# Two-head attention in value blocks of four steps, row maxima half a group ahead, and projection loads moved

## The reference

```
h = layernorm(x, g1, be1) * (1 + scale_msa) + shift_msa
q, k, v = split(h @ Wqkv + bqkv)                       # (B, S, H, HD) each
attn = softmax(einsum('blhd,bmhd->bhlm', q, k) * HD**-0.5, axis=-1)
h = einsum('bhlm,bmhd->blhd', attn, v).reshape(B, S, D) @ Wproj + bproj
x = x + gate_msa * h
x = x + gate_mlp * mlp(layernorm(x, g2, be2) * (1 + scale_mlp) + shift_mlp)
```

## Time and profile before

| | |
|---|---|
| the profiled execution's own time | 3572.36 us |
| its span | 3570.6 us |
| mean granted TensorE clock | 0.949 |
| TensorE matmul busy | 3329.7 us (93%) |
| VectorE busy | 2006.8 us (56%) |
| GpSimd busy | 1573.1 us (44%) |
| ScalarE busy | 1537.6 us (43%) |
| attention, first load to last store | about 886 to 2603 us |
| projection | about 2604 to 2845 us |

### The profile page before, as it was taken

One profiled execution on the slowest core, in us unless ns is written; L12 is line 12 of the kernel. 1 busy time (PEld: TensorE's weight loads), 2 busy tenths in 40 slices (PEclk: granted clock), 3 DMA queues, 4 the chain that ended last, 5 costly groups with the idle time before them and its releaser, 6 DMA issues. The chain is left out here.

```text
span 3570.6 us, 45393 instructions
## 1 busy us (share of the span) xinstructions
PE 3329.7 (93%) x17036; PEld 2237.9 (63%) x17036; DVE 2006.8 (56%) x3384; ACT 1537.6 (43%) x2790; POOL 1573.1 (44%) x590
## 2 busy tenths in 40 slices
PE   7989996998899999999999999999946699999999
PEld 6478885777455555555555555554324478888887
DVE  1278884443887877787777877775033332222222
ACT  0011113443056666666666666667613342222222
POOL 1033331000067887788777878778834200000000
PEclk9899997999599999999999999999967899999999
DMA  4222223444446776667766776666655431111100
GB/s 153 85 80 94 93 86 138 171 169 151 104 110 159 184 170 163 162 160 177 183 167 167 168 178 164 162 150 144 145 158 193 169 132 39 39 39 38 38 33 24
DMA packets 200487, 458.89 MB, mean 129 GB/s; under 512 B 61419, under 2 KB 83179, under 8 KB 169582
## 3 DMA queue, kind: packets, MB, share of 16 engines
q1 hardware_dynamic: 142126, 265.59, 22.3%
q0 software_dynamic: 18432, 134.23, 18.5%
q10 hardware_dynamic: 39744, 56.63, 6.1%
HBM read 165.71 MB, written 88.34 MB: 71 GB/s over the span
## 5 line engine op out<-in xcount | busy, mean ns | idle before, releaser
L1226 DVE TENSOR_REDUCE att_mx<-att_pM 128x1 f32<-128x512 f32 x2048 | 1249.4, 681 | 328.8 <-PE att_pM L1281 328.3
L1211 ACT ACTIVATE att_prob<-att_pS 128x512 f32<-128x512 f32 x2048 | 1040.3, 620 | 440.3 <-PE att_pS L1328 438.9
L1153 POOL TENSOR_TENSOR att_acc<-att_acc,att_prob 128x2048 f32<-128x2048 f32 x224 | 1029.8, 4597 | 204.5 <-ACT att_prob L1211 192.1
L1281 PE MATMUL att_pM<-att_ks,att_qs 96*128 96x512 f32 x2048 | 843.5, 426 | 21.3 <-DMA att_ks<-qk_d 21.2
L1328 PE MATMUL att_pS<-att_qs,att_ks 98*128 98x512 f32 x2048 | 844.3, 416 | 4.0 <-ACT att_prob L1211 3.7
L1328 PEld LDWEIGHTS att_pS<-att_qs,att_ks 98*128 98x128 f32 x2048 | 384.7, 189 | 350.1 <-issue 203.2
L1296 PE MATMUL att_pO<-att_prob,att_V 128*32 128x512 f32 x4096 | 497.4, 603 | 0.0
L1281 PEld LDWEIGHTS att_pM<-att_ks,att_qs 96*128 96x128 f32 x2048 | 404.7, 198 | 129.3 <-DVE att_mx L1226 52.4
L1782 DVE TENSOR_TENSOR mlp_us<-mlp_tu,mlp_us 128x512 fp32r<-128x512 f32 x128 | 89.7, 701 | 536.9 <-ACT mlp_us L1755 536.9
L1825 PE MATMUL mlp_pu<-mlp_hs,mlp_W 128*128 128x512 f32 x1536 | 371.1, 391 | 19.6 <-DVE mlp_W L1774 19.6
L1844 PE MATMUL mlp_pa<-mlp_W,mlp_us 128*128 128x512 f32 x1536 | 368.8, 389 | 0.0
(11 more groups left out here) (197 smaller groups left out, 3037.8 us busy)
## 6 DMA issues: line engine op xcount, KB each, us to landing
att_gathered<-att_prob POOLq DMA_DIRECT2D x128, 1024.0 KB, 7.9
att_gathered<-att_prob SPq DMA_DIRECT2D x64, 1024.0 KB, 4.7
qk_d<-qkv_qs SPq DMA_DIRECT2D x64, 512.0 KB, 2.7
att_qs<-qk_d ACTq DMA_DIRECT2D x39, 512.0 KB, 8.4
att_ks<-qk_d ACTq DMA_DIRECT2D x39, 512.0 KB, 7.5
gat_xT<-in_xT SPq DMA_DIRECT2D x32, 256.0 KB, 3.2
gat_xrow<-in_x SPq DMA_DIRECT2D x32, 256.0 KB, 2.8
x_d<-gat_x SPq DMA_DIRECT2D x32, 256.0 KB, 2.1
```

Source lines behind the costliest of these rows:

```text
L1153: nc.gpsimd.tensor_tensor(acc[half][:], old[:], new[:], ALU.add).then_inc(added, 1)
L1211: nc.scalar.activation(prob[step % PR][:, c, :], pS[at % 3][:], ACT.Exp, scale=SCALE).then_inc(exp_done, 1)
L1226: nc.vector.tensor_reduce(mx[:, q // 4, q % 4:q % 4 + 1], bank(at)[:], AX.X, ALU.max).then_inc(m_read, 1)
L1281: nc.tensor.matmul(bank(at)[:], qs[k][0:KD, h, t * P:(t + 1) * P], ks[k][0:KD, h, mc * 512:(mc + 1) * 512], start=True, stop=True).then_in ...
```

## The change

In attention: the values of four steps are made together (VB = 4) instead of two. The maxima are organised by half groups (n = 2g + half, NM = 64 tiles), and run half a group and six steps ahead, so that 64 + 24 tiles come before the first score and the first half of the last group still has maxima; `top_of`, `parts` and `rows` come twice per group, with 16 rows instead of 32, and `rows` is four DMAs instead of two. q and k have two buffers instead of three; their loads for group g + 1 are issued at steps 1, 2, 3, 5, 6 and 7 of group g, and V at step 8. Group 0's loads are split by head. In the memory that is freed, projection's weights, bias, gates and first chunk are loaded while attention runs. In projection, `of` and `zr` of chunk i + 2 are loaded when chunk i's low part is made; `xr` still behind chunk i's store.

```diff
-        NM = 2 * MT * 4
+        NM = MT * 4
-        U = 3
+        U = 2
+        VB = 4
-        LOADS = [3, 6, 9, 12, 15, 18]
+        LOADS = [1, 2, 3, 5, 6, 7]
...
         def m_tile(g, step, c):
-            ahead = 1 if step < ST - LEAD else 2
-            return (g + ahead, (step + LEAD) % ST * 4 + c) if g + ahead < NG else None
+            n, at = 2 * g + step // MT, step % MT
+            ahead = 1 if at < MT - LEAD else 2
+            return (n + ahead, (at + LEAD) % MT * 4 + c) if n + ahead < 2 * NG else None
...
+        def load_head(eng, h):
+            for i in range(6):
+                if i < 3:
+                    dst, src = qs[0][i * HD:(i + 1) * HD, h], q_v[(0, 0, 1)[i], 0, :, h, 0:S]
+                else:
+                    dst, src = ks[0][(i - 3) * HD:(i - 2) * HD, h], k_v[(0, 1, 0)[i - 3], 0, :, h, 0:S]
+                eng.dma_start(raw(dst), src).then_inc(head_loaded[h], 16)
...
-            def rows(g):
-                sp.wait_ge(m_read, turn(g) + 1)
-                for h in range(2):
-                    sp.dma_start(raw(qs[g % U][KD + h:KD + h + 1]).rearrange("a h (t n) -> a (h t) n", n=P),
-                                 raw(nm[:, h, :])).then_inc(top_rows[g % U], 16)
+            def rows(n):
+                g, half = divmod(n, 2)
+                sp.wait_ge(m_read, turn(n) + 1)
+                for w in range(2):
+                    for h in range(2):
+                        row = qs[g % U][KD + w:KD + w + 1, h, half * (S // 2):(half + 1) * (S // 2)]
+                        sp.dma_start(raw(row).rearrange("a (t n) -> a t n", n=P),
+                                     raw(nm[h * 8:(h + 1) * 8, w, :])).then_inc(top_rows[g % U], 16)
...
-            load(0)
+            load_head(sp, 0)
+            load_head(sp, 1)
+            load_v(0)
             load(1)
-            load_v(0)
             load_v(1)
-            load(2)
             rows(0)
+            for c in range(DC):
+                sp.dma_start(keep["p_stage"][:, c, :], io["Wproj"][c * P:(c + 1) * P, :]).then_inc(weights_early, 16)
...
+                if n == 2 * NG - 2:
+                    sp.wait_ge(o_stored, 64 * (2 * NG - 2))
+                    sp.wait_ge(z_kept, 32 * (2 * NG - 2))
+                    load_output(sp, io, 0, keep["p_of"], keep["p_zr"], first_o, first_z)
...
             def ahead(g, step):
-                if step == 1:
+                if g + 1 == NG:
+                    return
+                if step in LOADS:
+                    load_part(act, g + 1, LOADS.index(step))
+                if step == 8:
                     act.wait_ge(step_done, g * ST)
-                if step == 2 and g + 1 < NG:
                     load_values(act, g + 1)
-                if step in LOADS and g + 2 < NG:
-                    load_part(act, g + 2, LOADS.index(step))
...
-                    if step == ST - LEAD and g + 1 < NG:
-                        top_of(g + 1)
-                    if step == ST - LEAD + 1 and g + 1 < NG:
-                        parts(g + 1)
+                    if step % MT == MT - LEAD and n + 2 < 2 * NG:
+                        top_of(n + 2)
+                    if step % MT == MT - LEAD + 1 and n + 2 < 2 * NG:
+                        parts(n + 2)
...
-                        if c == 2 and step % 2 == 0 and (g or step):
-                            behind(*divmod(g * ST + step - 2, ST))
-                            behind(*divmod(g * ST + step - 1, ST))
+                        if c == 2 and step % VB == 0 and (g or step):
+                            for back in range(VB, 0, -1):
+                                behind(*divmod(g * ST + step - back, ST))
...
 def proj_phase(nc, io, keep):
-            load(0, 0)
...
+            load_o(1, 1)
+            load_x(0, 0)
...
+            load_x(1, 1)
+            for i in range(NCH):
+                s = i % 2
+                if i + 2 < NCH:
+                    sp.wait_ge(o_lo, DC + i)
+                    load_o(i + 2, s)
                 sp.wait_ge(x2_ready, i * 4 + 4)
                 sp.dma_start(io["x2_d"][bass.ds(i * 512, 512), :].rearrange("(n p) d -> p n d", p=P), x2[s][:]).then_inc(x_stored[s], 16)
-                if before(i, NCH - 2):
-                    load(i + 2, s)
+                if i + 2 < NCH:
+                    load_x(i + 2, s)
```

More of the change, by code:

```diff
@@ L1001, in attention_phase @@
             for step in range(ST):
-                if step == ST - LEAD + 1 and g + 1 < NG:
-                    fill(f"turned {g + 1}")
+                n = 2 * g + step // MT + 1
+                if step % MT == MT - LEAD + 1 and n < 2 * NG:
+                    fill(f"turned {n}")
                 for c in range(4):
@@ L1091, in keep_inverted @@
                     sp.dma_start(z_v[g // 2, h, g % 2, half], packed[h * 64:(h + 1) * 64, :]).then_inc(z_kept, 16)
-            load(0)
+            load_head(sp, 0)
+            load_head(sp, 1)
+            load_v(0)
             load(1)
-            load_v(0)
             load_v(1)
-            load(2)
             rows(0)
[L1099 to L1112, removed]
+            for c in range(DC):
+                sp.dma_start(keep["p_stage"][:, c, :], io["Wproj"][c * P:(c + 1) * P, :]).then_inc(weights_early, 16)
+            for b in range(B):
+                sp.dma_start(keep["p_gate"][b][:], io["gate_d"][0, b * (S // 512)]).then_inc(weights_early, 16)
+            sp.dma_start(keep["p_bp"][:], io["rows"][6:7, :].to_broadcast([P, D])).then_inc(weights_early, 16)
+            for n in range(2 * NG):
+                if n >= 1:
+                    store(n - 1)
+                send_first(n)
+                if n >= 1:
+                    pack(n - 1)
+                    keep_inverted(n - 1)
+                if n + 1 < 2 * NG:
+                    rows(n + 1)
+                if n == 2 * NG - 2:
+                    sp.wait_ge(o_stored, 64 * (2 * NG - 2))
+                    sp.wait_ge(z_kept, 32 * (2 * NG - 2))
+                    load_output(sp, io, 0, keep["p_of"], keep["p_zr"], first_o, first_z)
             store(2 * NG - 1)
@@ L1117, in _ @@
             sp.wait_ge(z_kept, 32 * 2 * NG)
+            sp.wait_ge(weights_early, 16 * (DC + B + 1))
+            sp.wait_ge(first_o, 16)
+            sp.wait_ge(first_z, 16 * DC)
         @block.gpsimd
@@ L1273, in _, with maxima, top_of @@
         def _(pe):
[L1274 to L1278, removed]
+            def maxima(n, q):
+                at, (g, half) = place[n, q], divmod(n, 2)
+                k = g % U
+                if n == 0 and q % 32 == 0:
+                    pe.wait_ge(head_loaded[q // 32], 96)
+                if half == 0 and q == 0 and g >= 1:
+                    pe.wait_ge(loaded[k], (g + k) // U * 96)
                 wait_bank(pe, at)
-                h, t, mc = q // 64, q // 4 % MT, q % 4
-                nc.tensor.matmul(bank(at)[:], qs[k][0:KD, h, t * P:(t + 1) * P], ks[k][0:KD, h, mc * 512:(mc + 1) * 512],
+                h, t, mc = q // 32, q // 4 % 8, q % 4
+                nc.tensor.matmul(bank(at)[:], qs[k][0:KD, h, (half * 8 + t) * P:(half * 8 + t + 1) * P], ks[k][0:KD, h, mc * 512:(mc + 1) * 512],
                                  start=True, stop=True).then_inc(m_done, 1)
[L1284 to L1287, removed]
+            def top_of(n):
+                pe.wait_ge(top_ready, n + 1)
+                wait_bank(pe, turn(n))
+                nc.tensor.transpose(bank(turn(n))[0:MT, 0:P], top[:], ident[:]).then_inc(m_done, 1)
             def values(g, step):
@@ L1374, in proj_phase @@
         ones2 = m.sb("ones2", [2, P], F32R)
-        zr = [m.sb(f"zr{i}", [P, DC, 512]) for i in range(2)]
+        zr = [keep["p_zr"], m.sb("zr1", [P, DC, 512])]
         os_ = [m.sb(f"os{i}", [P, 2, DC, 512], F32R) for i in range(2)]
@@ L1379, in proj_phase @@
         xn = m.sb("xn", [P, 4, D])
-        of = [m.sb(f"of{i}", [P, DC, 512]) for i in range(2)]
+        of = [keep["p_of"], m.sb("of1", [P, DC, 512])]
         ht = [m.sb(f"ht{i}", [P, 512]) for i in range(4)]
@@ L1402, in _, with load_o, load_x @@
         def _(sp):
[L1403 to L1412, removed]
-            load(0, 0)
-            sp.dma_start(bp[:], io["rows"][6:7, :].to_broadcast([P, D])).then_inc(b_loaded, 16)
-            sp.dma_start(gate[1][:], io["gate_d"][0, NB]).then_inc(g_loaded[1], 16)
-            load(1, 1)
+            def load_o(i, s):
+                load_output(sp, io, i, of[s], zr[s], o_loaded[s], z_loaded[s])
+            def load_x(i, s):
+                sp.dma_start(xr[s][:], io["x1_d"][bass.ds(i * 512, 512), :].rearrange("(n p) d -> p n d", p=P)).then_inc(x_loaded[s], 16)
+            load_o(1, 1)
+            load_x(0, 0)
             sp.wait_ge(bias_split, 2)
@@ L1874, in build @@
             qkv_phase(nc, io, keep)
-        if upto > 2:
-            attention_phase(nc, io, keep)
-        if upto > 3:
-            proj_phase(nc, io, keep)
+        with ExitStack() as early:
+            e = Mem(nc, early, "proj_early")
```

(9 more changed lines are left out.)

82 lines of the change are left out of this document (40 added, 42 removed).

## The result

| | before | after |
|---|---|---|
| median, side by side on one chip | 3568.74 us (3565.61 to 3572.8, 4 runs) | 3667.88 us (3658.92 to 3676.07, 4 runs) |
| ratio, with its 95% interval | | 1.0269 (1.0256 to 1.0283) |
| the profiled execution's own time, its span | 3572.36, 3570.6 | 3676.07, 3674.0 |
| mean granted TensorE clock | 0.949 | 0.942 |

The account below looks back on a forecast made before the run. It took TensorE to bound attention, VectorE attention's start and loads projection. Start -46, full groups +70, last group +5, loads +8 and projection -63 gave -26; the forecast was 3545 us, range 3505 to 3600.

Parts of the forecast that it names:

- The start: Attention before the first score: 64 fewer maxima tiles and a smaller first load, -46 us (-38 to -46).
- VectorE's lag: Full groups: VectorE falls behind TensorE in stretches of 16 pairs; with top and parts twice, +4.7 a group, +70 us.
- the +3.1: Net cost per full group of value blocks of four: 5.7 us of lag against 2.6 us fewer changes of tiling.
- the +1.6: Cost in us per full group of inverse, top part and split all falling into one late stretch in both halves.
- +0.6 a group, +8: Late k loads for the next group: TensorE's wait at step 10, +0.6 us a group, +8 in all (0 to +42).
- T + 34: Expected landing of the three k loads, in us after the group's first score, with gathers ending at T + 28.
- T + 38.5: Landing of the k loads if GpSimd's adding gathers take half the engines, costing +2 to +3 us a group.
- Rival 1: Attention's k loads come too late: slower from 2.9 us of waiting a group, 3605 us at 5; chance 0.2.
- Group 15: Last group: 64 maxima tiles in its first half, and longer blocks covering less of ScalarE's work, +5 us (+2 to +12).
- Projection: Early first chunk, -23 us, and earlier loads with chunks 20 us apart, -40; sum -63 us (-35 to -89).
- rival 2: Projection's loads stay the pace: 23 us gained at the start and 2 a chunk, 3573 us, no change; chance 0.12.
- Rival 3: Attention's value blocks of four: VectorE's lag is hidden, -2.6 us a group, -40 instead of +70, 3435 us; chance 0.05.

Follow-up runs that it names:

- e5: The kernel before with value blocks of four steps instead of two as its only edit: 3657.5 us, 1.0233 of before.
- e4: e1 with VectorE's maxima reductions over 256 of 512 columns, so not the same computation: 3434.29 us, 0.9603 of before.
- e1: The changed kernel with all six q and k loads issued at steps 0, 1 and 2, before the gathers: 3563.73 us, 0.9969 of before.
- e8: e1 with only the sixth load, of k, moved back to step 7: 3563.45 us, 0.9976 of before.
- e9: e1 with value blocks of two steps in the second half of group 15: 3552.72 us, 0.9944 of before.
- e2: The changed kernel with value blocks of two steps, its loads as they are: 3560.08 us, 0.9959 of before.

## Why the prediction was wrong

**The start** was right: first maxima tile at 895.39, first score at 948.06, -46.1 us.

**VectorE's lag** was right in mechanism and place, and nearly in size (+79 in groups 1 to 14, forecast +66). In a stretch of sixteen pairs the maxima tiles stand 0.60 us apart from about the tenth on, in place of 0.47, and each record is longer while it waits for its bank. In after:

```profile
1561.42 0.47 PE L1308 MATMUL att_pM<-att_ks,att_qs 96*128 96x512 f32 x1
...
1564.37 0.50 PE L1308 MATMUL att_pM<-att_ks,att_qs 96*128 96x512 f32 x1
...
1564.97 0.51 PE L1308 MATMUL att_pM<-att_ks,att_qs 96*128 96x512 f32 x1
1565.40 1.06 PE L1323 MATMUL att_pO<-att_prob,att_V 128*32 128x512 f32 x8
```

Second halves are 52.7 us (forecast 52.4). e5 shows it without the rest of the change, +4.7 a group; e4 removes it. The split was wrong: e5 has the inverse in both halves and `top_of` and `parts` in the second only, and its halves are 2.1 and 2.6 us longer than before. With all three in both halves (e1) a group is only 0.8 longer again. So the blocks cost more than the +3.1 that I gave them, and the second `top_of` and `parts` less than the +1.6.

**The loads are the step that failed,** the term "+0.6 a group, +8": both when they land and what a late one costs. The prediction read one load, 10.0 us behind two gathers, as "it ran after them, and before GpSimd's", and so let three loads and the gathers take their turns: T + 34, +0.6 a group. In after the gathers themselves landed 7.9 and 15.2 us after their issue, the 2 KB operands of the inverse in 16.4 and V in 27.1. With one load beside them, in group 6 before, the gathers took 4.5 and 7.9 and the 2 KB operands 8.5; in e1, with no load of q or k beside them, 4.7 and 6.8, the operands 4.5 and V 10.0. What SyncE's and ScalarE's queues had in flight became slow together, the engines being full (share 1.08); GpSimd's first two gathers took 13.2 and 10.4, no longer than the 14.4 and 14.0 before. That is sharing, not turns; the Trainium skill's rule (DMA: Bandwidth & Descriptors, Queues, rings and completion order), that the engines round-robin between the queues they have work for, fits these rows, and the prediction set it aside on the one row that couldn't tell: with a single load, order and sharing give nearly the same landing, and e8 shows that a single late load costs nothing in either reading.

The landing was the smaller part of the error. The first maxima tile that needs k starts at T + 37.0 to 40.2 (T is the group's first score), T + 38.4 on average, which is the T + 38.5 that the prediction worked out for GpSimd's gathers taking half the engines and priced at +2 to +3 a group. The wait for k is indeed 2.4. At that price the sum would have been about 0, no change. The loss is 8.1, because the prediction put at nothing what comes with that wait: the inverse's operand, late with the loads, and the clock.

Rival 1 was the one that came true, but not by its own count: it took the wait for k alone, with 2.9 us a group as the point of decision and 5 as its price, and that wait is 2.4 on average, 4.3 in group 5. It missed that the packed operand shares the same DMA engines and stands ahead of `top_of` (3.5 us of TensorE on average, 2.34 in group 5), and that TensorE comes back from the gap at half clock: in group 5 from 1540.88 to 1552.37, less the second wait, about ten pairs at 0.86 instead of 0.47 to 0.60, so 3 to 4 us. The three make some 10 us in this group, which is its 62.86 against the 53 of e1. With 8.1 in place of 0.6 the prediction's sum is -26 + 14 x 7.5 = +79, 3648 against the median, within 20 us of the result.

**Group 15:** +9 instead of +5, within its range (2 to 12) and so by luck: the half without maxima went from 49.9 to 56.5 us. I had priced the idle time behind ScalarE at +0.2 per four steps and not the clock. The window of this half in after, and of the value block that ends a long stretch in it:

```profile
2688.58:2745.07 56.49, 55.66 (x225) 19.04 (x224) 0.25 (x1) 32.55 (x66) 39.30 (x12) 0.77 0.60 149
...
2720.30:2726.20 5.90, 5.90 (x34) 1.50 (x34) 0.25 (x1) 0.77 (x2) 4.18 (x2) 0.64 0.99 196
```

A four-step block lasts 3.64 us at full clock and 5.4 to 5.8 here, granted 0.64 in the second line. Before, this half was granted 0.93, and e9 gets 0.95 with blocks of two. After's first half took 50.6, where the forecast had 52.4: it gave this half all 64 maxima tiles of the last half, but VectorE has 40 there (its window counts 48 instructions, a full half 69), the other 24 being made in group 14's last six steps.

**Projection** was right. From the last score to chunk 1: -23 (forecast -23). Per chunk 21.6 us (129.3 over six, 2791.51 to 2920.85), forecast 20, 26.7 before. GpSimd's timeline shows the first chunk without a wait for `zr`, and the third, which still has one, half of the 19.90 before:

```profile
2763.86 6.71 POOL L1542 TENSOR_TENSOR proj_early_of<-proj_early_of,proj_early_zr 128x512 f32<-128x512 f32 x4
...
2802.00 4.60 POOL L1533 TENSOR_TENSOR proj_early_of<-proj_early_of,proj_early_zr 128x2048 f32<-128x2048 f32 x1 [10.55 <-DMA proj_early_zr<-z_d]
```

So the loads are still the pace, inside the 20 to 24 that the prediction gave for them; chunks gain 5.1 us each, not the 2 of rival 2. Rival 3 (the blocks bring what they should) is ruled out by e5.

**Left open.** Of the 8.1 us a group the two waits are 2.4 and 3.5, less the 0.5 that the transpose waits in e1 too; how the rest divides between half clock and what VectorE catches up meanwhile isn't measured. Nor is what makes the same late loads land early in three of e2's groups and late in the others.

## What to carry to other kernels

Before moving a load, list everything that is in flight in the 15 us behind its new place and treat it all as sharing the DMA engines, small transfers too; then look what is queued behind each that becomes late, and test the issue steps alone, since the six numbers in LOADS were worth 104 us here. A wait is priced with what queues behind it and with the clock after it, not by its own length: 2.4 us of waiting for k went with a loss of 8.1. A longer stretch on one engine is only as good as the number of buffers times the pace difference of its partner allows: at 0.470 against 0.599 us with four banks it is ten tiles, not sixteen. A change with parts of both signs is worth taking apart: two of this one's four parts, the start and projection, gave 46 and 54 us, the other two took more than that, and without them the kernel is 2.7% faster than before.

## What the runs showed of the hardware that I had not expected

- 2 KB transfers queued behind two 1 MB gathers, beside three 512 KB loads, landed in 16.4 us, with one load in 8.5 and with none in 4.5, so a small operand pays for large neighbours.
- The granted clock fell where no single long gap stood before it. In group 15 TensorE ran one score tile for each exponential of ScalarE (about 0.49 us) through a four-step stretch, and the value block behind it was granted 0.64; with two-step stretches the half kept 0.95.
- After a gap of 4.30 us TensorE ran at 1.2 GHz for the following 11.5 us, with a second gap of 2.34 us in them. After gaps of 0.8 us (e2, groups 1, 2 and 8) the half kept a granted clock of 1.00.
